# The FFN stage of a fused embedding, attention and FFN kernel, its steps put in another order

## The reference

```python
def rmsnorm(x, g):
    return x * rsqrt(mean(x * x, axis=-1) + 1e-6) * g
def act_quant(x):                     # per row
    scale = 127.0 / clip(max(abs(x), axis=-1), 1e-05, None)
    return clip(round(x * scale), -128.0, 127.0) / scale
def weight_quant(w):                  # to -1, 0, 1 times one step
    scale = 1.0 / clip(mean(abs(w)), 1e-05, None)
    return clip(round(w * scale), -1.0, 1.0) / scale
def bitlinear(x, w, g):
    return einsum('bsd,fd->bsf', act_quant(rmsnorm(x, g)), weight_quant(w))
def ffn(x):
    return bitlinear(gelu(bitlinear(x, w1, g1)), w2, g2)      # 192 -> 768 -> 192
h = h + ffn(layernorm(h))
```

## Time and profile before

| | |
|---|---|
| time, median of 3 runs | 1753.07 us (1752.8 to 1753.71) |
| the profiled execution: its own time | 1751.31 us |
| its span, first to last instruction | 1749.6 us |
| busy over the span: PE, DVE | 1473.4 us (84%), 1461.2 us (84%) |
| busy over the span: ACT, POOL | 1232.4 us (70%), 1099.7 us (63%) |
| mean granted TensorE clock | 0.913 |

### The profile page before, as it was taken

One profiled execution on the slowest core, in us unless ns is written; L12 is line 12 of the kernel. 1 busy time (PEld: TensorE's weight loads), 2 busy tenths in 40 slices (PEclk: granted clock), 3 DMA queues, 4 the chain that ended last, 5 costly groups with the idle time before them and its releaser, 6 DMA issues.

```text
span 1749.6 us, 53766 instructions
## 1 busy us (share of the span) xinstructions
PE 1473.4 (84%) x18602; PEld 1203.6 (69%) x18602; DVE 1461.2 (84%) x3227; ACT 1232.4 (70%) x1862; POOL 1099.7 (63%) x1369
## 2 busy tenths in 40 slices
PE   5799999999999999999999999985556565656565
PEld 2688888888888888888888888874454454544454
DVE  5588888888888888888888888874899999999996
ACT  0476666667676776767667676653688888888887
POOL 5456565656666665666665656542777777777775
PEclk9899999999999999999999999996677877777876
DMA  8533334343434343434343333320000000000000
GB/s 209 78 60 68 61 63 65 61 67 60 68 60 68 59 69 55 72 53 74 53 72 56 70 58 68 60 56 18 9 24 20 24 20 24 20 24 20 24 20 29
DMA packets 104194, 93.57 MB, mean 53 GB/s; under 512 B 22737, under 2 KB 94466, under 8 KB 104162
## 3 DMA queue, kind: packets, MB, share of 16 engines
q1 hardware_dynamic: 103394, 91.58, 27.7%
q0 software_dynamic: 768, 1.57, 0.4%
HBM read 74.12 MB, written 11.91 MB: 49 GB/s over the span
## 4 chain that ended last, share of the span: by engine, by line
PE 66%; DVE 20%; issue 7%; ACT 3%; POOL 1%; DVEq 1%; DMA 0%; SPq 0%; ACTq 0%; POOLq 0%
PE ps L1039 19%; PE ps L1096 9%; PE ps L1182 8%; DVE nmax L677 6%; PE ps L1173 5%; PE ps L1129 5%; DVE ff_st L813 4%; PE ps L1280 3%; PE ps L1161 3%; PE ps L1155 3%; PE ps L1261 3%; PE ps L1134 2%; PE ps L1077 2%; PE ps L1110 2%; DVE xpix L806 1%
## 5 line engine op out<-in xcount | busy, mean ns | idle before, releaser
L1039 PE MATMUL ps<-w_eff,pix 124*112 124x193 f32 (+1 forms) x2048 | 406.8, 337 | 10.4 <-DMA pix<-side 8.4
L677 DVE TENSOR_REDUCE nmax<-ps 116x12 bf16<-116x1344 f32 (+2 forms) x192 | 302.9, 1577 | 87.1 <-PE ps L1134 87.1
L493 POOL TENSOR_TENSOR pix<-probs,g_b 112x192 f32<-112x192 f32 (+1 forms) x512 | 298.0, 612 | 103.5 <-ACT probs L994 94.2
L882 ACT ACTIVATE probs<-ps,isw 116x688 f32<-116x688 f32 x384 | 298.9, 831 | 84.6 <-PE ps L1161 83.2
L1039 PEld LDWEIGHTS ps<-w_eff,pix 124*112 124x112 f32 (+1 forms) x2048 | 308.3, 167 | 37.2 <-issue 22.0
L420 POOL TENSOR_TENSOR xsq<-xsq 124x784 f32<-124x784 f32 (+1 forms) x128 | 184.4, 1441 | 216.1 <-ACT xsq L875 211.1
L440 POOL TENSOR_SCALAR_AFFINE_SELECT probs<-probs 116x464 f32<-116x464 f32 x384 | 274.1, 726 | 68.9 <-ACT probs L882 60.4
L1250 PE MATMUL ps<-ident_h,xpix 112*96 112x112 f16 (+1 forms) x256 | 34.9, 281 | 193.8 <-DVE xpix L830 187.9
L864 ACT ACTIVATE pix<-xpix 54x896 f32<-54x896 f32 (+1 forms) x128 | 196.6, 1538 | 1.2 <-DMA xpix<-in_x 0.4
L1096 PE MATMUL ps<-xnT,wq_pad 97*128 97x228 f32 (+1 forms) x768 | 166.5, 366 | 0.0
L1250 PEld LDWEIGHTS ps<-ident_h,xpix 112*96 112x96 f16 (+1 forms) x256 | 23.8, 167 | 205.0 <-issue 103.3
(11 more groups left out here) (134 smaller groups left out, 3175.1 us busy)
## 6 DMA issues: line engine op xcount, KB each, us to landing
xpix<-in_x SPq DMA_DIRECT2D x192, 196.0 KB
rden<-den_rows SPq DMA_DIRECT2D x256, 85.5 KB, 2.2
out<-xpix SPq DMA_DIRECT2D x64, 87.0 KB
out<-xpix SPq DMA_DIRECT2D x64, 84.0 KB
xpix<-in_x SPq DMA_DIRECT2D x128, 34.1 KB
h_all<-shift_w SPq DMA_DIRECT2D x5, 768.0 KB, 4.4
pix<-side SPq DMA_DIRECT2D x64, 36.8 KB
pix<-side SPq DMA_DIRECT2D x64, 36.6 KB
```

The lines of the kernel that those rows point to most:

```text
L493: last = nc.gpsimd.tensor_tensor(v2[0:P, b, tile, cols], gel[0:P, b, tile, cols], g2_b[0:P, cols], ALU.mult)
L677: V.tensor_reduce(dst, src, AX_X, ALU.max, negate=True).then_inc(s_mx, 1)
L882: A(probs[0:TB, g, 2 * e:2 * e + 2, :], ps[0:TB, 4 + 2 * e:6 + 2 * e, 0:SK], ACT.Exp, scale=isw[0:TB, 7:8]).then_inc(s_p, 1)
L1039: last = MM(ps_tok[tile][0:P, :], pix[0:HI, par, o, lo:lo + P], w_eff[0:HI, o, :], start=(o == 0), stop=(o == OFFS - 1))
```

## The change

DVE. The row statistics of an image are made one step earlier (`row_variation`, `row_moments`, `row_mean_squares`), with a semaphore `f_row` of their own in place of links, and are put between other instructions. A step begins with centring, which waits for q1 of the step before. The product with the weight step (L822) leaves the chain; `weigh_steps` does it in the next step and raises `f_step`, on which gelu and the rows `y` wait. The mean square of gelu comes after `y` instead of before centring, and the two maxima of `v2` wait for their tiles one by one. Links in a step: 5 instead of 7.

ACT. The order becomes quantise, first copy, squares (of the image of the step before), second copy, gelu. PE. The order becomes first turn, second turn, first product, second product, and the second product now belongs to the same image as the second turn, one step earlier than before. A call at the end goes.

Besides, `ln_st` is 40 instead of 32 columns wide, the attention stage's POOL function gets a parameter that it doesn't use, and an `if` is split in two. The diff, cut to the FFN stage:

```diff
+            def row_variation(m, b):      # these four functions are new
+                apart(dve)
+                for tile, P in enumerate((TA, TB)):
+                    ins = V.bn_stats(ff_st[0:P, b, 6 * tile:6 * tile + 6], h_all[0:P, hcols(m, tile)])
+                ins.then_inc(f_row, 1)
+            def row_moments(m, b):
+                dve.wait_ge(f_row, 2 * m + 1)
+                apart(dve)
+                for tile, P in enumerate((TA, TB)):
+                    ins = V.bn_aggr(ff_st[0:P, b, 12 + 2 * tile:14 + 2 * tile], ff_st[0:P, b, 6 * tile:6 * tile + 6])
+                ins.then_inc(f_row, 1)
+            def row_mean_squares(m, b):
+                dve.wait_ge(f_row, 2 * m + 2)
+                return V.tensor_scalar(ff_st[:, b, 16:18], ff_st[:, b, 13:16:2], 1.0 + EPS_RMS, EPS_LN * EPS_RMS, ...)
+            def weigh_steps(i, b):
+                after(dve, f_g, 2 * i)
+                V.tensor_tensor(ff_st[:, b, 40:44], ff_st[:, b, 28:32], w_step[:, :], ALU.mult).then_inc(f_step, 1)
...
 DVE  def ffn_step(i, b, new=True, mid=True, last_=True, steps_=True, coming=True, skipped=0):
-                if new or mid:
-                    after(dve, f_g, 2 * i)
-                    after(dve, f_q2, i - 2)
-                if new:
-                    (bn_stats, link, bn_aggr, link, mean square of m)
-                if mid:
-                    dve.wait_ge(f_ssq, 2 * j + 2)
-                    (mean square of gelu)
+                if new:
+                    after(dve, f_q1, m)
+                    dve.wait_ge(f_row, 2 * m + 2)
                     (centring of m)
+                if coming:
+                    row_variation(m + 1, 1 - b)
                     (maxima of v1)
+                if coming:
+                    row_moments(m + 1, 1 - b)
+                if steps_:
+                    weigh_steps(i - 1, 1 - b)
+                if coming:
+                    first = row_mean_squares(m + 1, 1 - b)
                 if last_:
+                    dve.wait_ge(f_step, o + 3)
                     dve.wait_ge(f_m2, o + 1)
                     (rows y of o)
+                if new or mid:
+                    after(dve, f_q2, i - 2)
                 if mid:
-                    dve.wait_ge(f_v2, 2 * j + 2)
+                    dve.wait_ge(f_ssq, 2 * j + 2)
+                    (mean square of gelu).then_inc(f_var, 1)
                     for tile: 
+                        dve.wait_ge(f_v2, 2 * j + tile + 1)
                         (maximum of v2)
                 (link, wait for f_r1, L819, link, L820, link, L821, link)
-                    V.tensor_tensor(st[:, 40:44], st[:, 28:32], w_step[:, :], ALU.mult)
                 (L823, q1)
...
 ACT  def ffn_step(i, b, new=True, mid=True, squares=True):
+                if mid:
+                    quantise(i, b, 0)
+                    quantise(i, b, 1)
                 if new:
                     (copy of the first transposes)
-                if mid:
-                    quantise(i, b, 0)
-                    quantise(i, b, 1)
-                if new:
-                    (gelu of m)
+                if squares:
+                    after(act, f_var, i + 1)
+                    (squares of image i)
                 if mid:
                     (copy of the second transposes)
                 if new:
-                    (squares of m)
+                    after(act, f_v2, 2 * m - 2)
+                    act.wait_ge(f_step, m + 1)
+                    (gelu of m)
...
 PE   def ffn_step(i, new=True, mid=True):
                 if new:
                     turn_first(i + 1)
-                if last_:
-                    ffn_second(i - 2)
+                if mid:
+                    turn_second(i - 1)
                 if new:
                     ffn_first(i + 1)
                 if mid:
-                    turn_second(i - 1)
+                    ffn_second(i - 1)
```

More of the change, by code:

```diff
@@ L763, in flink @@
                 dve.wait_ge(f_vc, flinks[1] + flinks[0])
-            def ffn_step(i, b, new=True, mid=True, last_=True, skipped=0):
+            def row_variation(m, b):
[9 more added lines that the diff above has]
+                ins.then_inc(f_row, 1)
@@ L976, in quantise, with ffn_step @@
                     ins.then_inc(f_q2, 1)
-            def ffn_step(i, b, new=True, mid=True):
+            def ffn_step(i, b, new=True, mid=True, squares=True):
                 m, j = i + 1, i - 1
+                if mid:
+                    quantise(i, b, 0)
+                    quantise(i, b, 1)
                 if new:
@@ L1004, in ffn_step @@
                 if new:
-                    after(act, f_var, m - 1)
+                    after(act, f_v2, 2 * m - 2)
+                    act.wait_ge(f_step, m + 1)
                     for tile, P in enumerate((TA, TB)):
-                        act.wait_ge(f_g, 2 * m + tile + 1)
-                        A(gsq[0:P, tile, :], gel[0:P, 1 - b, tile, :], ACT.Square,
-                          accum_out=gel_sum[0:P, 1 - b, tile:tile + 1]).then_inc(f_ssq, 1)
-            ffn_step(-1, 1, mid=False)
+                        act.wait_ge(f_m1, 2 * m + tile + 1)
+                        A(gel[0:P, 1 - b, tile, :].rearrange("p (c d) -> p c d", c=2),
+                          ps[0:P, 2 + 2 * tile:4 + 2 * tile, 0:HIDDEN // 2], ACT.Gelu,
+                          scale=ff_st[0:P, b, 40 + tile:41 + tile]).then_inc(f_g, 1)
+            ffn_step(-1, 1, mid=False, squares=False)
             act.wait_ge(s_h2, IMAGES)
@@ L1021, in _ @@
             ffn_step(IMAGES - 1, 1, new=False)
-            ffn_step(IMAGES, 0, new=False)
+            ffn_step(IMAGES, 0, new=False, squares=False)
         @block.tensor
@@ L1308, in _ @@
             ffn_step(IMAGES, new=False)
-            ffn_step(IMAGES + 1, new=False, mid=False)
 def shape_constants():
```

78 lines of the change are left out of this document (39 added, 39 removed).

## The result

The kernel after took 1707.48 us (median of 4 runs, 1704.58 to 1708.7), the kernel before 1752.93 on the same chip: ratio 0.974, 95% interval 0.9723 to 0.9756. The forecast was 1750.7 with a range of 1733 to 1767. The time lies outside it, and 45 us have to be accounted for. The profiled execution of after has a span of 1704.6 us (before 1749.6).

A forecast was written before the change was run, and what follows sets the result against it. DVE was taken to bound the FFN steps: its own work plus holds under POOL's products. 61 x (7.93 - 7.96) = -1.8, start-up -1.0, end +0.4: total -2.4, giving 1750.7 us, range 1733 to 1767.

The forecast's parts named there:

- part 3: DVE's new order, timed from the scales' end: centring ends at 2.0, y begins 3.6 to 3.9, root product at 6.55.
- part 4: DVE's root product under POOL's first product at 6.13: three held instructions, 1.70 to 1.89 us, period 7.83 to 8.02.
- Part 1: ACT's new order, inputs in time: gelu begins 5.16 us after the scales, POOL's first product at 6.13.
- faster rival: Root product starts before POOL's first product, two holds follow: steps of 7.4 mixed with 7.9, 1733.6 us; chance 0.26.
- The weight step's removal "gives nothing": DVE's chain before the scales: no gain, the scales instruction is held instead; if it were not, 0.29 to 0.48 less.
- Part 2: PE's turns ahead of its products: only ACT waits for them, cost 0; y's wait goes, 0 to 0.19 us saved.
- Start-up and end: Outside the 61 periods: image 1's statistics made during the attention wait, -1.0 us; last gelu behind squares, +0.4 us.
- the two widest gaps in the earlier trace: Centring's new wait for q1's end on DVE: upper bound 0.32 us, from gaps of 0.13 and 0.19 added.
- The rules weighed: Skill rules: DVE semaphores cost nothing extra, where the trace showed 0.15 us; GpSimd contends with Vector instructions of two SBUF inputs.

The follow-up runs named there:

- root product later: Kernel after plus a spare DVE maximum over 192 columns between the maxima of v2 and the root product: 1727.26 us, ratio 0.9856.
- statistics in their step: Kernel after with row statistics, moments and mean square back in the image's own step, ahead of centring: 1761.38 us, ratio 1.0045.
- folded kernels: After with the clip folded into neighbouring instructions, 1692.72 us; the same with row mean squares behind gelu mean squares, 1689.4; before with the clip folded, 1732.3.

## Why the prediction was wrong

**The step that failed** is the last term of part 3: "the root product (L819) begins between 6.3 and 6.8; I take 6.55". It begins at 5.99 and 6.03, ahead of POOL's product. So part 4's three holds became two, and its step of 7.83 to 8.02 became 7.21 and 7.29. All its mistakes above 0.02 have one sign (the step shown above):

| term | predicted | measured |
|---|---|---|
| q1 ends | 0.85 | 0.87 |
| centring ends | 2.0 (1.6 to 2.3) | 1.87 |
| statistics, maxima, aggregation end | 3.25 | 3.07 |
| weight step held, ends | 3.5 | 3.45 |
| y begins | 3.6 to 3.9 | 3.45 |
| gelu mean squares begin | 4.3 to 4.6 | 4.10 |
| maxima's time | 1.80 | 1.81 |
| link to the root product | 0.13 | 0.03 |
| root product begins | 6.55 | 6.03 |

The 0.52 can be taken apart, to a hundredth or two. The largest term, 0.25, is what was put between the weight step and y (3.75, the middle of its bounds, less 3.5): y begins as the weight step ends, so the mean squares, the waits and the address instructions there cost nothing. The link gave 0.10: its 0.13 was read from the earlier trace rows, where L819 stood behind maxima that ended at 1515.91, and here the same pair has a gap of 0.03. Another 0.09 is the gelu mean squares, counted at their full 0.17 although the maxima begin 0.08 after them (1459.54 and 1459.62 above). The weight step's end and the time from y to the gelu mean squares gave 0.05 each. That centring was 0.13 early did not count, since the weight step is held to the end of a product that is on from 2.83 to 3.43 in the timeline. The low end, 6.3, was still 0.3 too late: a range for a sum of this many terms has to be wider.

**Part 1, ACT's order: right.** POOL's first product was forecast at 6.13 and came at 6.05 and 6.13. That decided the case together with the failed term: the root product was to be 0.4 late and is early, by 0.03 and 0.14.

**Part 4, where the two meet: the mechanism was right, its size for this case was the rival's.** Clip and scales are held to the ends of the first and of the second product. From POOL's start to the end of the scales it is 1.16 us; the rival had 0.59 + 0.72 = 1.31, which counted a product begun late that was not late. 6.05 + 1.16 = 7.21, 6.13 + 1.16 = 7.29: the two step lengths. The faster rival was therefore the right case, and it was mixed wrongly: I had half the steps go each way (7.65, 1733.6 us, still 26 us too slow), but only two of 61 root products were held (0.24 and 0.37 us, near 1250 and 1258 us), and the other 59 were free. The reason is seen in "root product later": whether one instruction is ahead of another is either the same in all steps or changes in a fixed turn. A mean over "hit" and "miss" is the length of no step.

**The weight step's removal "gives nothing"**: right but for 0.06 a step. That the scales instruction would then be held itself: right (median 293 ns).

**Part 2, PE's order "cost 0"**: right for the pair, but the question was too narrow. In the kernel before, PE's new order alone costs 179 us (1932.89 against 1753.52 on that chip); with DVE's and PE's new orders and ACT's old one it is 1928.37, with DVE's and ACT's new ones and PE's old one 1824.94. The prediction did not work out what each would do without the other, and so did not see that this is the part with the highest price for a mistake.

**Start-up and end:** -1.0 and +0.4 forecast; -2.2 and 0 measured, no matter.

**Two slips that changed nothing.** 61 x -0.13 to +0.06, with -0.6, from 1753.07 is 1744.5 to 1756.1, not 1746 to 1757. And "the two widest gaps in the earlier trace rows" leaves out the 0.15 that the same paragraph uses.

**The rules weighed.** With a link the root product begins 0.03 behind the maxima's end; without one, neighbours overlap by 0.07 to 0.08 (row mean squares begin at 1458.81, before the weight step's end at 1458.89). And the 0.15 behind statistics is real, as "statistics in their step" shows again. The rule of the Trainium skill (VectorE: DVE Perf Modes, "The DRAIN you can't avoid") that a semaphore costs nothing extra is borne out at neither place, though the link to the root product costs less than my 0.13. No run took a link away and left the rest alone. In each second step the first centring instruction takes 0.63 us under a product, the pair 0.96, and yet the pair ends at the same 1.87, since there it begins at 0.91 and not at 1.12. On this the trace agrees with the Trainium skill's rule on instructions with two SBUF inputs (GPSIMD Engine Reference, "Key points").

**What stays open.** Why the hold lets an instruction through that begins 0.02 us behind POOL's and not one that begins 0.10 behind is only seen. Nor is it a fixed allowance: in "statistics in their step" the row mean squares begin 0.01 behind a product and are held 0.61. Nor is it settled which instruction sets off the long step in the folded kernels.

## What to carry to other kernels

When two engines get in each other's way, an instruction's cost is a step function of which of them is first: write down the lead (here 0.03 to 0.14 us), not a mean. When it is smaller than the error of the sum, forecast the two step lengths as two cases and do not mix them. Take instructions out from behind the edge rather than from in front of it: one clip gone there gave 15 us, while y 0.45 us earlier in front of it gave nothing. And before calling a queue order free, work out the ring with only that engine changed: an order that fits its partner can be ruinous without it.

## What the runs showed of the hardware that was not expected

- An independent four-column instruction between two linked ones was free: it filled the time in which the second waits (1461.29 and 1461.40 above). One of 0.33 us was not.
- GpSimd's product does not scale with its columns: 0.39 us for 96, 0.59 for 192, 0.99 for 384 where nothing disturbs it. That is some 0.18 us fixed (an estimate from the three). Of two DVE instructions back to back under it, the second is not held, and POOL's product is stretched instead (0.84 us in the timeline of after, where q1's second half ran under it and centring began). Which of them stretches it was not tried.
- GpSimd's roots of four columns took 1.01 us beside DVE's maxima, and 1.43 in a step of the kernel before, beside centring.
- Between 1300 and 1600 us TensorE's mean granted clock was 0.76 in after, and 0.55, 0.57 and 0.56 with PE's order old, with ACT's order old, and for before with PE's order new: mostly the lower of its two levels (1.2 GHz). PE waits there 1.1 to 2.5 us at a time, on average, ahead of a turn or a product. The second turns take 1.3 us in nearly all their steps, and 0.8 in 17 of 41 steps of after. How much of those kernels' long steps is the slower PE was not taken apart.
